# A three-block decoder on one core: stacks by one-hot products, early rows for two expert tiles, a changed order of steps

## The reference

```
attention:  q, k, v = x @ qkv_w.T ; q, k to unit length over all 128 channels
            16 heads of 8; softmax(q k / (8 * temperature)) v ; projection
cross:      q from x, k and v from the context, each with a bias; 16 heads of 8
            softmax((q k + skew(q Er)) / sqrt(8)) v, causal, Er 256 x 8
experts:    logits = x @ router_w + router_b ; top = argmax
            h = x @ w1[top] + b1[top] ; a, g = split(h)
            y = (a * sigmoid(g)) @ w2[top] + b2[top]      (8 experts, 512 wide)
```

## Time and profile before

| what | value |
|---|---|
| median of 3 runs | 324.76 us (322.9 to 327.62) |
| the profiled execution | 320.35 us |
| its span | 318.6 us |
| mean granted TensorE clock in it | 0.917 of full |
| busy: PE, DVE, ACT, POOL | 234.0, 208.4, 125.5, 69.4 us |

### The profile page before, as it was taken

The page is one execution under the profiler, slowest core; times in us unless marked ns, Lnnn a source line. Parts: engine busy times, 40 slices in busy tenths (PEclk is TensorE's granted clock), DMA queues, the critical chain, the costliest instruction groups (busy, mean ns, idle before and its releaser), DMA issues.

```text
span 318.6 us, 8169 instructions
## 1 busy us (share of the span) xinstructions
PE 234.0 (73%) x3285; PEld 167.2 (52%) x3285; DVE 208.4 (65%) x579; ACT 125.5 (39%) x286; POOL 69.4 (22%) x105
## 2 busy tenths in 40 slices
PE   4327587666998979999769989536875399999650
PEld 1102132313675666667548776326774249999650
DVE  6479774798658866686886645627342455998680
ACT  3220066401884228755226675202443204444230
POOL 2302011081020002122010130003010020555543
PEclk9999999975899979999999999955899679999995
DMA  2480077753588651079670227250113032863800
GB/s 63 143 200 20 2 249 234 196 121 56 181 245 291 141 112 69 2 208 286 135 170 5 85 42 190 66 120 19 37 35 101 0 75 60 242 228 124 230 6 1
DMA packets 28533, 38.18 MB, mean 120 GB/s; under 512 B 4567, under 2 KB 22213, under 8 KB 27728
## 3 DMA queue, kind: packets, MB, share of 16 engines
q1 hardware_dynamic: 24432, 25.50, 32.5%
q0 software_dynamic: 4064, 12.16, 11.4%
HBM read 25.46 MB, written 12.59 MB: 119 GB/s over the span
## 4 chain that ended last, share of the span: by engine, by line
PE 34%; DMA 22%; DVE 22%; issue 6%; ACT 5%; POOL 5%; SPq 4%; POOLq 0%; DVEq 0%; ACTq 0%
DVE negm L881 5%; SPq L403 4%; PE SB L1196 4%; PE SA L1305 4%; PE SB L1192 3%; PE MB L1069 3%; DMA w_sb<-parts_a 3%; PE SB L1305 3%; DMA parts_a<-SpA 3%; PE MA L1069 2%; DMA sorted_x<-P2b 2%; PE SA L1106 2%; PE SB L1313 2%; DMA x_tok<-in_x_rows 2%; DMA Z<-parts_b 2%
## 5 line engine op out<-in xcount | busy, mean ns | idle before, releaser
L881 DVE TENSOR_REDUCE negm<-SA 128x2 bf16<-128x512 f32 x64 | 41.6, 691 | 4.8 <-PE SA L1106 3.5
L688 ACT ACTIVATE P<-SA 128x512 f32<-128x512 f32 x64 | 35.6, 605 | 3.5 <-PE SA L1121 2.0
L941 DVE TENSOR_REDUCE negm<-MB 128x4 bf16<-128x512 bf16 x32 | 22.0, 688 | 13.2 <-PE MB L1069 13.1
L646 ACT ACTIVATE Sb<-SB 128x512 bf16<-128x512 f32 x24 | 14.3, 596 | 39.6 <-PE SB L1196 39.6
L1106 PE MATMUL SA<-KS,QS 96*128 96x256 bf16 x64 | 16.0, 357 | 9.0 <-DMA KS<-parts_a 6.7
L936 DVE TENSOR_TENSOR Sm<-SB,Sb 128x512 bf16<-128x512 f32 x16 | 11.0, 689 | 17.1 <-ACT Sb L646 17.1
L719 ACT ACTIVATE P2b<-SB 128x1024 f32<-128x1024 f32 x16 | 16.4, 1028 | 9.8 <-PE SB L1215 7.9
L1106 PE MATMUL SA<-w_sb 96*128 96x256 bf16 x64 | 13.9, 313 | 7.0 <-DVE negm L881 4.9
L1215 PE MATMUL SB<-identb,negm 128*128 128x128 bf16 x192 | 17.1, 231 | 1.3 <-DVE negm L941 1.3
L602 POOL TENSOR_TENSOR rs<-ve,half 128x2 f32<-128x2 f32 x8 | 5.7, 713 | 53.4 <-DVE ve L845 53.4
L646 ACT ACTIVATE P<-MA 128x128 f32<-128x128 f32 x15 | 4.2, 278 | 32.8 <-PE MA L1069 32.8
...
## 6 DMA issues: line engine op xcount, KB each, us to landing
...
```

Of the source, the lines that this page charges most:

```text
L646: return a.activation(dst, src, ACT.Copy)
L688: a.activation(P1[:, grp % 2, kt, 2 * i:2 * i + 2, :].rearrange("p h t -> p (h t)"), SA[:, bank_a("st", b, u), :], ACT.Exp).then_inc(s["ex ...
L881: v.tensor_reduce(out=negm1[:, qt, :, hp], in_=SA[:, bank_a("d", b, u), :].rearrange("p (g k) -> p g k", g=2), axis=AX.X, op=ALU.max, nega ...
L941: v.tensor_reduce(out=negm2[:, qb, :], in_=MBb[:, 0:512].rearrange("p (c k) -> p c k", c=4), axis=AX.X, op=ALU.max, negate=True).then_inc( ...
```

## The change

Batch 0's stack comes from PE: `stack_heads` multiplies the three terms by one-hot tables, `stacked` copies the result out (ACT); new steps `ex0` to `ex7`, one for a pair of heads. Its tables are built by DVE at the start, in place of memsets that go to POOL. The stack's columns are laid out anew (`column_a`), so that a half of them gets its shifts at once: `shT` becomes `shT0` (after the eighth maximum) and `shT1`. In batch 3 queries 0 to 127 are stacked by PE as well (`stack_queries`, steps `gt0`, `gt1`, 64 queries each, with a table that POOL builds in step `pk0` in the room of expert weights 5 to 7, which are therefore loaded later); only queries 128 to 255 go through DRAM and under the mask. Tiles 0 and 1 take the rows of batches 0 to 2 from an early load and those of batch 3 by products with one-hot slots. All seven further tiles have rooms of their own. The warming products are spread over four places. `ORDER` is another list. The diff, cut:

```diff
-STAGES = 4
 OUTS = 4
 BLANK_PIECES, BLANK_ROWS = 4, 9
-WARMING = 18
+WARMING = {"nm1": 8, "x2T": 1, "lg": 3, "rk": 3}
+AT_ONCE = 2
 
...
-    A1.qkv.0 A1.qkn.0 A1.vcp.0 A1.qkT.0 A1.k5.0 A1.qkv.1 A1.qsin.0 A1.k2.0 A1.d0.0 A1.d1.0 A1.d2.0 A1.d3.0
...
+    A1.k2.0 A1.qkv.0 A1.vcp.0 A1.k1.1 A1.qkn.0 A1.qkT.0 A1.k5.0 A1.qkv.1 A1.ex0.0 A1.ex1.0 A1.d0.0 A1.d1.0
+    A1.ex2.0 A1.ex3.0 A2.cx.0 A1.d2.0 A1.d3.0 A2.xpb.0 A1.d4.0 A1.d5.0 A1.ex4.0 A1.d6.0 A1.d7.0 A1.ex5.0 A1.d8.0
+    A1.d9.0 A1.shT0.0 A1.ex6.0 A1.d10.0 A1.d11.0 W.bl0.0 A1.ex7.0 A1.d12.0 A1.d13.0 W.v6.0 A1.d14.0 A1.d15.0
...
+    A2.st0.1 A2.st1.1 A1.shT1.1 B.build.0 A2.st2.1 A2.st3.1 A2.st4.1 A2.st5.1 A2.st6.1 A1.qkT.2 A2.st7.1
+    B.rest.0 A2.pv0.1 A2.pv1.1 A2.st8.1 A2.cx.1 B.sc0.0 A2.nm0.1 A2.st9.1 A2.st10.1 B.tr0.0 B.sc1.0 A2.st11.1
...
+    B.v.3 B.gt0.3 B.sc0.3 B.ln2.2 B.gt1.3 B.tr0.3 B.sc1.3 B.sc2.3 B.sh0.3 W.u5.0 W.u6.0 B.rest.3 B.tr1.3 W.u7.0
+    B.sc3.3 B.tr2.3 B.sh1.3 B.sh2.3 B.tr3.3 B.sc4.3 W.v3.0 W.v4.0 B.x2T.2 B.sh3.3 B.tr4.3 B.sc5.3 B.sh4.3 B.lg.2
+    B.tr5.3 W.v5.0 B.sc6.3 B.sh5.3 B.tr6.3 B.sc7.3 B.pv0.3 B.sh6.3 B.tr7.3 B.rk.2 B.sh7.3 B.nm0.3 B.pv1.3
+    B.nm1.3 B.ln2.3 B.x2T.3 B.lg.3 B.rk.3
...
+def column_a(g, j):
+
+    return 8 * (j // 4) + 4 * g + j % 4
...
+        PICKS = 3 * H * SR
+        picks = flatP2b[:, BLANK_ROWS * ROW:BLANK_ROWS * ROW + PICKS].bitcast(BF16)
+        pick_q, pick_k = (picks[:, i * PICKS:(i + 1) * PICKS].rearrange("p (w j m) -> p w j m", w=3, m=2 * SR) for i in range(2))
+        WIDE = 2 * 64 - 2 * D
+        wide_picks = w1_sb[:, 5:8, :].rearrange("p e t -> p (e t)").bitcast(BF16)[:, 0:3 * H * WIDE]
+        pick_both = wide_picks.rearrange("p (w h m) -> p w h m", w=3, h=H)
+        odd_rows = sb("odd_rows", [P, 1])
...
             def q_k_out(b):
-                wait(sp, "qs_in", b * 64)
+                if b == 0:
+                    return
+                wait(sp, "qs_in", (b - 1) * 64)
...
-            def shift_rows(b):
-                sp.wait_ge(s["ma_free"], a_full(b, "shiftT"))
-                sh = shift_a[b]
-                load(sh.rearrange("q h t -> (q h) t"), nmT[:, :], "m_out")
-                sp.wait_ge(s["m_out"], b * 16 + 16)
-                load(QSs[b % 2][96:97, :, :].rearrange("o h (q t) -> o h q t", q=TT), sh.rearrange("q h t -> h q t").unsqueeze(0), "m_in")
+            def shift_rows(b, a):
+
+                sp.wait_ge(s["ma_free"], a_full(b, f"shiftT{a}"))
+                sh = shift_a[b, a]
+                load(sh.rearrange("q h t -> (q h) t"), nmT[:, a, :], f"m_out{a}")
+                sp.wait_ge(s[f"m_out{a}"], b * 16 + 16)
+                load(QSs[b % 2][96:97, 8 * a:8 * a + 8, :].rearrange("o h (q t) -> o h q t", q=TT), sh.rearrange("q h t -> h q t").unsqueeze(0), f"m_in{a}")
 
...
+                q = OTHERS if b == NB - 1 else slice(0, NT)
                 for half_ in (0, 64):
-                    load(Zs[b % 2][half_:half_ + SR, :, :], stack(parts_b, 0), "qz_in")
+                    load(Zs[b % 2][half_:half_ + SR, :, q], stack(parts_b, 0)[:, :, q], "qz_in")
...
+            sp.wait_ge(s["ma_full"], a_full(NB - 1, "pv1"))
+            sp.wait_ge(s["scat"], scattered(NB - 1))
+            for e in range(AT_ONCE):
+                load(early_rows[:, e, :], sorted_x[e * REGION:e * REGION + SLOTS, :], "early_in")
...
-                if d >= STAGES:
-                    wait(sp, "down_full", E + d - STAGES + 1)
-                    wait(sp, "res3_ok", E + d - STAGES + 1)
-                load(more_w1[d % STAGES], one(w1[bass.ds(e, 1)]), f"more_in{d % STAGES}")
-                load(more_w2[d % STAGES], one(w2[bass.ds(e, 1)]), f"more_in{d % STAGES}")
-                load(more_b2[:, d % STAGES, :], one(b2[bass.ds(e, 1), :]).partition_broadcast(P), f"more_in{d % STAGES}")
+                load(more_w1[d], one(w1[bass.ds(e, 1)]), f"more_in{d}")
+                load(more_w2[d], one(w2[bass.ds(e, 1)]), f"more_in{d}")
+                load(more_b2[:, d, :], one(b2[bass.ds(e, 1), :]).partition_broadcast(P), f"more_in{d}")
...
+            link(g.memset(QS0[:, :, :].rearrange("p h t -> p (h t)").bitcast(U32), 0))
+            link(g.memset(KS0[:, :, :].rearrange("p h t -> p (h t)").bitcast(U32), 0))
+            g.memset(KS0[96:97, :, :].rearrange("p h t -> p (h t)").bitcast(U32), 0x3F803F80).then_inc(s["stack0_fill"], 1)
+            pool.wait_ge(s["stack0_fill"], 1)
+            link(g.memset(odd_rows[:, :], 1.0))
+            g.affine_select(out=odd_rows[:, :], in_=odd_rows[:, :], compare_op=ALU.is_gt, fill=0.0,
+                            base=1 - SR, pattern=[[0, 1]], channel_multiplier=1).then_inc(s["odd_ok"], 1)
+            pool.wait_ge(s["odd_ok"], 1)
+            link(g.memset(V1[:, :, :, :], 0.0))
+            g.memset(V1[:, :, :, D:D + 1], 1.0).then_inc(s["v1_fill"], 1)
...
+            def picks_of_both(b, k):
+
+                paced(f"pk{k}")
+                link(g.memset(wide_picks.bitcast(U32), 0))
+                of_heads = identb[:, :].rearrange("p (d h) -> p h d", h=H)
+                for part, first, past, step in ((0, 0, 3, 1), (1, 3, 6, 2), (2, 4, 5, 1)):
+                    for at in (0, 64):
+                        blocks = pick_both[:, part, :, at:at + SR].rearrange("p h (k d) -> p h k d", d=D)[:, :, first:past:step, :]
+                        link(g.tensor_copy(blocks, of_heads.unsqueeze(2).broadcast_to(blocks.shape)))
+                pool.sem_inc(s["both_ok"], 1)
+
...
+                if e >= 5:
+                    pool.wait_ge(s["gt_full1"], 2)
...
+            def root2(b, _):
+                if b == NB - 1:
+                    pool.wait_ge(s["ma_full"], a_full(b, "pv1"))
+                    g.iota(slot_no[:, :, :], pattern=[[REGION, AT_ONCE], [1, P]], base=0, channel_multiplier=0, allow_small_or_imprecise_dtypes=True)\
+                        .then_inc(s["slot_no_ok"], 1)
+                    pool.wait_ge(s["slot_no_ok"], 1)
+                root(rs2[:, :], ve2[:, :], "ve2_ok", "rs2_ok", b + 1)
+
             def scatter_rows(b):
+                if b == NB - 1:
...
+            def stacked(b, hp):
+
+                if hp == 0:
+                    act.wait_ge(s["stack0_fill"], 1)
+                    act.wait_ge(s["odd_ok"], 1)
+                act.wait_ge(s["ex_full"], hp + 1)
+                room = SB[:, hp % 4, :]
+                copy(QS0[0:SR, column_a(0, hp), :], room[0:SR, 0:NT])
+                a.activation(QS0[0:2 * SR, column_a(1, hp), :], room[0:2 * SR, 0:NT], ACT.Copy, scale=odd_rows[0:2 * SR, :])
+                copy(KS0[0:2 * SR, hp, :], room[0:2 * SR, NT:2 * NT]).then_inc(s["ex_out"], 1)
...
+            def first_heads(b, n):
+
+                if n == 0:
+                    act.wait_ge(s["sc_full"], (b - 1) * NQB)
+                act.wait_ge(s["gt_full0"], n + 1)
+                to, room = Zs[b % 2][:, 0:H // 2, 64 * n:64 * n + 64], SA[:, 0, :].rearrange("p (h q) -> p h q", q=64)
+                copy(to[0:SR, :, 0:64:2], room[0:SR, :, 0:64:2])
+                copy(to[64:64 + SR, :, 1:64:2], room[64:64 + SR, :, 1:64:2]).then_inc(s["first_ok"], 1)
...
-            link(v.memset(words(QS0), 0))
-            link(v.memset(words(KS0), 0))
-            v.memset(words(KS0[96:97, :, :]), TWO_ONES).then_inc(s["fill"], 1)
+            link(v.memset(picks.bitcast(U32), 0))
+            dve.wait_ge(s["consts"], 1)
+
+            def pick(table, part, first, past, step):
+
+                for g in range(2):
+                    blocks = table[:, part, :, g * SR:(g + 1) * SR].rearrange("p j (k d) -> p j k d", d=D)[:, :, first:past:step, :]
+                    of_heads = identb[:, :].rearrange("p (d g j) -> p g j d", g=2, d=D)[:, g, :, :]
+                    ins = v.tensor_copy(blocks, of_heads.unsqueeze(2).broadcast_to(blocks.shape))
+                return ins
+
+            pick(pick_q, 0, 0, 3, 1)
+            pick(pick_q, 1, 3, 6, 2)
+            pick(pick_q, 2, 4, 5, 1)
+            pick(pick_k, 0, 2, 5, 1)
+            pick(pick_k, 1, 0, 6, 5)
+            pick(pick_k, 2, 1, 2, 1).then_inc(s["pick_ok"], 1)
             dve.wait_ge(s["temp_in"], 16)
             link(v.reciprocal(temp[:, :], temp[:, :]))
             link(v.tensor_scalar(trow[:, :, :], temp[:, :].unsqueeze(1).broadcast_to([P, D, H]), 1.0 / D, None, ALU.mult))
...
+            def last_heads(b, n):
+
+                if n == 0:
+                    dve.wait_ge(s["sc_full"], (b - 1) * NQB)
+                dve.wait_ge(s["gt_full1"], n + 1)
+                to, room = Zs[b % 2][:, H // 2:H, 64 * n:64 * n + 64], SA[:, 1, :].rearrange("p (h q) -> p h q", q=64)
+                v.tensor_copy(to[0:SR, :, 0:64:2], room[0:SR, :, 0:64:2])
+                v.tensor_copy(to[64:64 + SR, :, 1:64:2], room[64:64 + SR, :, 1:64:2]).then_inc(s["last_ok"], 1)
...
+                    dve.wait_ge(s["slot_no_ok"], 1)
+                    for e in range(AT_ONCE):
```

(53 more changed lines are left out.)

203 lines of the change are left out of this document (116 added, 87 removed).

## The result

The changed kernel took 312.5 us (median of 4, 311.56 to 315.33) beside 323.83 (median of 4) of the kernel before on the same chip: ratio 0.968, 95% interval 0.959 to 0.978. The forecast was 311.8. The profiled execution fell from 320.35 to 311.56 us, its span from 318.6 to 309.8, by 8.8 us.

What follows compares the result with a forecast made beforehand. PE was taken to bound the middle, with time lost at the ends and one place between. Terms 4 + 2.5 + 3.4 + 3.1 = 13.0 us off 320.35 gave 307.4, plus 4.4 to the median: 311.8 us, range 303 to 320.

Steps and rivals of the forecast that it cites:

- Opening and middle: Everything before the last query projection (203.75 us): 4 us gained, bounds 8 and minus 4.
- I take 0.22: Opening on DVE: each of 12 one-hot table copies takes 0.22 us, 2.6 us in all.
- what PE does there it needn't do after 80: Batch 1's transposed scores fill some 8 us of idle PE before 80 us, relieving the PE-bound middle; 8 if wholly used.
- Rival (b): Middle: cross-attention chain is the bound, a late B.sc0.0 gives minus 4 instead of plus 4; 319.8 us, chance 0.16.
- The last batch's queries: Batch 3's queries stacked by PE instead of through DRAM: net 2.5 us gained, ends minus 12.4 and plus 7.7.
- 5.05 + 96p: Batch 3's third score block starts at 208.8 + 96p us, against 220.43 before.
- The term p: Batch 3's queries: one product with its weight load, taken as 0.094 us for 112 columns.
- delays one transpose's maximum by some 0.7: Between batch 3's score blocks: DVE's choice (1.4 us) for batch 2 delays one transpose's maximum by some 0.7 us.
- stay up: Batch 3's queries: PE works through the gap, so the clock stays up and gives 0.6 us back.
- First tiles: First expert tiles, up to tile 2's first product: 3.4 us gained through early rows and warming products.
- If it is low at 255, tile 0 runs at half rate ... 1.75: First tiles, low clock at 255 us: tile 0 at half rate, tile 2 starts at 264.9, gain 1.75 us.
- Weights of tiles 8 to 14: Last expert tiles: with seven rooms no waits for weights at tiles 12 and 13; 3.1 us gained, ends 0 and 3.1.

Runs made afterwards that it cites:

- experiment 1: Changed kernel with POOL's memsets held back until DVE's twelve copies of the one-hot tables are done; ratio 0.972 to the kernel before.
- experiment 8: Changed kernel with weights of tiles 12 to 14 loaded only once tiles 8 to 10 are done with their buffers; ratio 0.981 to the kernel before.
- experiment 2: Changed kernel with two key steps (k2 of batch 0, k1 of batch 1) moved out of the opening; median 306.31 us, 0.954 of the kernel before.
- experiment 6: Changed kernel with batch 0's first transposed score waiting for both halves of the maxima rows; ratio 0.988 to the kernel before.
- experiment 11: Changed kernel with two key steps out of the opening, a 128-column query table and more warming products; median 306.12 us, 0.945 of the kernel before.
- experiment 12: Kernel of experiment 11 with one load of up weights moved behind batch 1's fourth pair of heads; median 303.76 us, 0.946 of the kernel before.
- Experiment 3: Changed kernel with the one-hot table of the last batch's queries at 128 columns instead of 112; ratio 0.972 to the kernel before.
- experiment 4: Changed kernel with 17, 2, 6 and 5 warming products instead of 8, 1, 3 and 3; median 311.29 us beside 320.93 of the kernel before.
- experiment 5: Changed kernel with batch 0's stack again written to DRAM and loaded back, PE's stacking of it removed; ratio 0.979 to the kernel before.
- Experiment 7: Changed kernel with tiles 0 and 1 waiting for rows loaded by DMA, without the products with one-hot slots; ratio 0.983 to the kernel before.

## Why the prediction was right, and where it wasn't

The time came within 0.7 us of the median, but the sum was too large by 4.2 us, and an error in the step from the profiled execution to the median hid it.

*Opening and middle, 4 us said, 1.56 measured.* Two steps failed. First, "I take 0.22" for a copy: 0.46 beside POOL's memsets, 0.19 without them (experiment 1). The first maximum came 1.5 us later than I had it. Second, what I added for the stretch in which PE idles, "what PE does there it needn't do after 80". Batch 1's stack, "about 1.7 us earlier", came 1.6 us earlier. PE was busy for more of the stretch:

```profile
60.00:80.00 20.00, 14.91 (x64) 0.57 0.50 123
...
100.00:150.00 50.00, 42.94 (x760) 0.91 0.49 130
150.00:200.00 50.00, 45.72 (x885) 0.95 0.33 71
```

```profile
60.00:80.00 20.00, 12.06 (x104) 0.70 0.57 104
...
100.00:150.00 50.00, 44.49 (x772) 0.97 0.53 140
150.00:200.00 50.00, 43.42 (x867) 1.00 0.46 108
```

These are the windows of PE after the change and, below, before it (busy, clock). It is busy 2.85 us more between 60 and 80, but at a lower clock: busy time times clock is 8.5 us after and 8.4 before, so by this estimate the idle stretch was filled with slower work and not with more. Between 100 and 200 the clock is lower again (0.91 and 0.95 against 0.97 and 1.00). What this second loss costs, experiment 8 shows: with the clock of the kernel before (0.97 and 1.00) its projection came at 200.43, 3.3 us earlier than before the change. So 1.8 us of the missing 2.4 went with the clock, for which the forecast had no term. Why it fell there is open, and with one trace of the kernel before and a spread of 200.4 to 207.2 us after, the stage's gain can't be given closer. Rival (b), a late B.sc0.0 setting the rest, isn't seen: that block came at 80.75 and 80.70 us (experiment 8), and in both the projection was still early.

I also had no step that says how an opening gain travels, and when I made one up (experiments 2 and 6), it was wrong: 4.8 us won at the first maximum gave 5.6 at the projection, 5.3 lost at the first transposed score took 5.2. That neither was lost on the way stands, by the whole times too (experiments 2, 6, 11 and 12); the sizes are given by single traces.

*The last batch's queries, 2.5 said, 2.23 measured.* The form, 5.05 + 96p behind the projection (208.8 less 203.75), is right: 6.63 us of products give 11.68, measured 11.64. The term p was not: 0.055, 0.069 over both groups, against 0.094. By the Trainium skill (TensorE: Matmul & The Clock Gate, Weight-path perf modes) the fast load needs 128 weights. Experiment 3 agrees that 128 columns load faster than 112 (0.0375 us against 0.055 at the full clock); what failed is the price I put on the slow case, from float32 rows. So the third block gained 5.0 us and not 2.6. The second error is "delays one transpose's maximum by some 0.7" for the work of batch 2 that had lain in the wait: from the fifth block to the second product with the values it took 20.65 us instead of 17.60, and 3.05 of the 5.0 went, for that work and for a clock that read 0.50 from 228 to 232 us where it had read 1.00. Nor did the clock "stay up": it halved in the second group. The third block's gain was 2.4 us larger than said and the loss behind it 2.3 us larger, which nearly cancels; that 2.5 and 2.23 are close is luck.

*First tiles, 3.4 said, 1.73 measured.* The prediction named both cases, 4.4 if the fillers hold the clock, and "If it is low at 255, tile 0 runs at half rate ... 1.75", and its 3.4 leans to the first, which didn't come. Where the clock read 1.00 at the first tile (experiments 4, 5, 6, 11, 12) it is 15.72 less 11.6 to 11.9, so 3.8 to 4.1. Experiment 7 shows that the early rows carry it: without them the stage takes 3.6 us more.

*Weights of tiles 8 to 14, 3.1 said, 3.25 measured*, and 2.1 of it seen to go when the ring is restored.

The sum missed by 4.2 us against the profiled execution (307.4 said, 311.56 measured). The prediction then added the 4.4 us by which the median of the kernel before lay above its profiled execution; for the changed kernel it was 0.9, and these 3.5 us brought the miss back to 0.7. The forecast was right in sign and range, its closeness is luck.
